# Decoder layer on one core: float32 products on raw data for the first two head pairs, and copies of products placed among the weight splits

## The chip, the cores and the metric

The kernel runs on one core of a Trainium2 chip. The metric is the device time in microseconds of one execution. Beside it one execution was taken by the hardware profiler; times within the kernel are microseconds from the start of that execution's span. The engines are PE (TensorE; PEld is its weight load), DVE (VectorE), ACT (ScalarE), POOL (GpSimd) and SP (SyncE, which only issues transfers here).

## The reference

One decoder layer over x of 8 batches x 128 tokens x 128 features, float32, with layer norms after each part:

```python
x = layernorm(x + self_attention(x))          # 16 heads of 64, causal
x = layernorm(x + cross_attention(x, ctx))    # 16 heads of 8, masked, with biases
x = layernorm(x + mixture(x))                 # 8 experts of 256, top-2 gates, all computed

# the part that matters here, in self_attention:
q = einsum('bsd,hqd->bhsq', x, w_q)
k = einsum('bsd,hqd->bhsq', x, w_k)
v = einsum('bsd,hvd->bhsv', x, w_v)
weights = softmax(causal(einsum('bhsq,bhtq->bhst', q, k)) / sqrt(64))
```

## The kernel before

All five engines run programs of their own, each in an order written out by hand, and wait for one another on semaphores. Batches are taken in pairs of 256 tokens for the q and k projections; p counts the eight pairs of heads (128 columns of w_q and of w_k each). `first_qk(p, b)` projects the first pair of batches into the PSUM bank b, q in its first 256 columns and k in its last 256; `next_qk` does the later pairs of batches, `project_v` one batch and half of the columns of w_v.

A projection is a split product. Each float32 operand is written as a rounded part (hi, in the format fp32r) and the rest (lo), and three fast products are summed: hi x hi, hi x lo, lo x hi (`split_product`, L1443 to L1445). The splitting is shared out:

- POOL splits x, two batches at a time: `split_x(k)` casts `x_hi` (L287) and subtracts `x_lo` (L289).
- ACT rounds the weights: `round_w(part)` (L515) writes `w_hi` and scales q's weights by 1/8. There are nine parts: columns 0 to 255 of q, of k, columns 256 to 511 of q, of k, and so on, and last the 1024 columns of w_v.
- DVE subtracts: `lower_w(part)` (L806) writes `w_lo`.

PE may start p = 2 when `w_lo_done` has reached 4, p = 4 at 6 and p = 6 at 8. Before its first projection PE multiplies a zeroed tile, `x1`, with itself WARM = 10 times (L1611). Copies of a product out of PSUM are shared by ACT (even p, L535) and DVE (odd p, L900). ACT does its eight roundings, then copies p = 0 and p = 2, then rounds w_v, then copies p = 4. DVE does eight subtractions, copies p = 1 and p = 3, subtracts w_v, then takes the maxima of the first two groups of scores (`group_max`, L839), copies v (`evac_v`, L915) and so on. `score_s(0, 0)` needs the copies of p = 0 to 3; `score_s(0, 1)`, in the bank OC from which `evac_v(0, 1)` copies, waits for that copy (`v_evac[1]`) and for the copies of p = 4 to 7. Scores go through `group_max`, `exp` (ACT, L525), a reciprocal (DVE, L846), `normalise` (POOL, L311) and `turn` (a transpose on PE, L1545).

Transfers go out in the order in which SP and ACT issue them: SP loads the first 256 tokens of xT, w_k's first columns, w_q's other three, w_v, the rest of xT, ctx, small weights and w_o. ACT loads w_q's first columns, w_k's other three, later the mask and x. When all nine lower parts are done SP issues the expert weights into the same memory.

PE's order is:

```python
for i in range(WARM): pe.matmul(OC[:, 0:P], x1[:], x1[:], start=True, stop=True)
first_qk(0, Y1); first_qk(1, OS); first_qk(2, T0); first_qk(3, T1)
first_qk(4, Y0); first_qk(5, X0)
score_s(0, 0, Y1, T1)
first_qk(6, X1)
project_v(0, 0, OS)
pe.wait_ge(maxed["s"][0], 1)
first_qk(7, Y1); next_qk(0, 0, T0)
project_v(0, 1, OC)
```

It goes on with `next_qk(0, 2)`, `next_qk(0, 3)`, `score_s(0, 1)`, `turn("s", 0, 0)`, `project_cv` (L1497, float32 products of 128 columns), and further on `turn("s", 2, 0)` and `turn("s", 3, 0)`, which stand at 23.1 us.

Of the kernel before, what the change touches and what calls it, by code (L numbers as in the profile page):

```python
# [9 lines left out]
ALU = mybir.AluOpType  # L10
ACT = mybir.ActivationFunctionType
AX_X = mybir.AxisListType.X

P = 128
# [24 lines left out]
def build_decoder(nc, x, xT, ctxT, mask, wqT, wkT, wvT, woT, cwqT, cwkT, cwvT, cwoT, cbq, cbk, cbv, cbo,  # L39
# [22 lines left out]
    W_PARTS = [(i, cols) for cols in W_COLS for i in (0, 1)] + [(2, slice(0, 1024))]  # L62
    NWP = len(W_PARTS)
    WARM = 10
# [9 lines left out]
    with ExitStack() as ctx:  # L74
# [3 lines left out]
        def sem(name):  # L78
            return ctx.enter_context(nc.semaphore(name))
# [130 lines left out]
        def hid_of(b):  # L210
            return max((j + 1 for j in range(NFILL) if FILL_BANK[j] is b), default=0)

        ld_xT, ld_xT_rest, ld_wv, ld_cwk, ld_cwq, ld_x, ld_ctx, ld_mask, ld_wo, ld_cw, ld_gu, ld_down = [
            sem(f"ld_{n}") for n in "xT xT_rest wv cwk cwq x ctx mask wo cw gu down".split()]
# [7 lines left out]
        ld_wqk = [sem(f"ld_w{'qk'[i]}{k}") for k in range(len(W_COLS)) for i in (0, 1)]  # L222
# [26 lines left out]
        def _(sp):  # L249
            sp.dma_start(xT_all[:, 0:2 * S], xT[:, 0:2 * S]).then_inc(ld_xT, 16)  # L250
            sp.dma_start(w_raw[:, 1, W_COLS[0]], wkT[:, W_COLS[0]]).then_inc(ld_wqk[1], 16)
            for k in range(1, len(W_COLS)):
                sp.dma_start(w_raw[:, 0, W_COLS[k]], wqT[:, W_COLS[k]]).then_inc(ld_wqk[2 * k], 16)
            sp.dma_start(w_raw[:, 2, :], wvT).then_inc(ld_wv, 16)
            sp.dma_start(xT_all[:, 2 * S:B * S], xT[:, 2 * S:B * S]).then_inc(ld_xT_rest, 16)
# [13 lines left out]
            sp.wait_ge(w_lo_done, NWP)  # L269
            sp.dma_start(gu_raw[:, 0, :], gateT).then_inc(ld_gu, 16)  # L270
# [12 lines left out]
        def _(pool):  # L283
            def split_x(k):
                toks = slice(2 * k * S, 2 * (k + 1) * S)
                pool.wait_ge(ld_xT if k == 0 else ld_xT_rest, 16)
                pool.tensor_copy(x_hi[:, toks], xT_all[:, toks]).then_inc(x_split, 1)  # L287
                pool.wait_ge(x_split, 2 * k + 1)
                pool.tensor_tensor(x_lo[:, toks], xT_all[:, toks], x_hi[:, toks].bitcast(F32), ALU.subtract).then_inc(x_split, 1)  # L289
# [217 lines left out]
        def _(act):  # L507
# [4 lines left out]
            def round_w(part_of):  # L512
                i, cols = W_PARTS[part_of]
                act.wait_ge((*ld_wqk, ld_wv)[part_of], 16)
                act.activation(w_hi[:, i, cols], w_raw[:, i, cols], ACT.Copy, scale=W_SCALE[i]).then_inc(w_hi_done, 1)  # L515
# [16 lines left out]
            def evac_first_qk(p, b):  # L532
                act.wait_ge(qk_first, p + 1)
                dst = qk_b[:, :, p % 4, :] if p >= 4 else qk_a[:, 0, :, p, :]
                act.copy(dst, b[:].rearrange("p (a c) -> p a c", a=2)).then_inc(qk_first_a, 1)  # L535
# [58 lines left out]
            round_w(1)  # L594
            round_w(2)
            round_w(3)
            round_w(4)
            round_w(5)
            round_w(6)
            round_w(7)  # L600
            evac_first_qk(0, Y1)
            evac_first_qk(2, T0)
            round_w(8)
            evac_first_qk(4, Y0)
# [193 lines left out]
        def _(dve):  # L798
# [4 lines left out]
            def lower_w(part_of):  # L803
                i, cols = W_PARTS[part_of]
                dve.wait_ge(w_hi_done, part_of + 1)
                dve.scalar_tensor_tensor(out=w_lo[:, i, cols], in0=w_raw[:, i, cols], scalar=W_SCALE[i],  # L806
                                         in1=w_hi[:, i, cols].bitcast(F32), op0=ALU.mult,
                                         op1=ALU.subtract).then_inc(w_lo_done, 1)
# [88 lines left out]
            def evac_first_qk(p, b):  # L897
                dve.wait_ge(qk_first, p + 1)
                dst = qk_b[:, :, p % 4, :] if p >= 4 else qk_a[:, 0, :, p, :]
                dve.tensor_copy(dst, b[:].rearrange("p (a c) -> p a c", a=2)).then_inc(qk_first_v, 1)  # L900
# [148 lines left out]
            lower_w(1)  # L1049
            lower_w(2)  # L1050
            lower_w(3)
            lower_w(4)
            lower_w(5)
            lower_w(6)
            lower_w(7)
            evac_first_qk(1, OS)
            evac_first_qk(3, T1)
            lower_w(8)
            dve.wait_ge(consts, 3)
            group_max("s", 0, 0, Y1)  # L1060
            group_max("s", 1, 0, T1)
            evac_v(0, 0, OS)
# [377 lines left out]
        def _(pe):  # L1440
# [13 lines left out]
            def first_qk(p, b):  # L1454
                if p == 0:

                    for a in range(2):
                        dst, cols = b[:, a * 2 * S:(a + 1) * 2 * S], slice(0, P)
                        pe.wait_ge(w_hi_done, a + 1)
                        pe.wait_ge(x_split, 1)  # L1460
                        pe.matmul(dst, w_hi[:, a, cols], x_hi[:, 0:2 * S], start=True, stop=False)
                        pe.wait_ge(x_split, 2)
                        pe.matmul(dst, w_hi[:, a, cols], x_lo[:, 0:2 * S], start=False, stop=False)
                        pe.wait_ge(w_lo_done, a + 1)
                        last = pe.matmul(dst, w_lo[:, a, cols], x_hi[:, 0:2 * S], start=False, stop=True)
                    last.then_inc(qk_first, 1)
                    return
                if p % 2 == 0:
                    pe.wait_ge(w_lo_done, p + 2)
                project_qk(0, p, b).then_inc(qk_first, 1)  # L1470
# [6 lines left out]
            def project_v(n, c, b):  # L1477
                if n == 0:
                    pe.wait_ge(w_lo_done, NWP)
# [638 lines left out]
```

## Time and profile before

| | |
|---|---|
| median of 3 runs | 233.37 us (233.29 to 233.5) |
| profiled execution, its own time | 233.06 us |
| its span | 231.0 us |
| PE, DVE, ACT, POOL busy | 98%, 83%, 71%, 44% |
| granted TensorE clock | 1.0 in the whole span |

A row of the timeline gives the start, the time from the first start to the last end of the instructions merged into it, the engine, the line of the kernel, the operation with what it writes and reads, how many instructions were merged, and in square brackets how long the engine had been idle before and who released it. PE's products overlap, so the pace of its stream is read from starts, not from lengths. A float32 product appears as two passes, each with a weight load.

### The profile page before, as it was taken

The page shows a single profiled execution, that of the slowest core. Times are in us where ns is not written, and L with a number is a line of the kernel's source. Part 1 is how long each engine was busy: PE and PEld are TensorE (multiplying, and loading weights), DVE is VectorE, ACT ScalarE, POOL GpSimd, SP SyncE. Part 2 cuts the span into 40 slices and gives each one's busy share as a digit, 9 for nine tenths or more (in the row PEclk, how much of TensorE's full clock was granted, in tenths as well). Part 3 has the DMA queues.
Part 4 walks back from the last instruction along what each step waited for, and adds up shares of the span by engine and source line. Part 5 has one row for each costly group of instructions (what it writes and reads, how often), then busy time and mean ns, then how long its engine had stood idle before and what let it go on. Part 6 is the DMA issues. An engine that isn't in the chain of part 4 may idle for free.

```text
span 231.0 us, 6982 instructions
## 1 busy us (share of the span) xinstructions
PE 225.9 (98%) x2274; PEld 205.9 (89%) x2274; DVE 192.1 (83%) x954; ACT 164.9 (71%) x552; POOL 102.0 (44%) x162
## 2 busy tenths in 40 slices
PE   8999999999999999999999999999999999999992
PEld 8999888997978988978978988789999999999992
DVE  3897798997889889989899879989898565766984
ACT  3768988898999979999989999697476333333001
POOL 4387738796396568922978351231200000100112
PEclk9999999999999999999999999999999999999999
DMA  6998000000000000000002200000000000000000
GB/s 189 362 363 314 10 0 0 4 3 1 3 1 3 0 6 3 0 3 1 1 4 64 121 3 3 3 0 4 0 3 0 1 3 0 4 23 0 26 23 24
DMA packets 7011, 9.10 MB, mean 39 GB/s; under 512 B 1088, under 2 KB 5824, under 8 KB 6592
## 3 DMA queue, kind: packets, MB, share of 16 engines
q1 hardware_dynamic: 4320, 7.09, 8.7%
q10 hardware_dynamic: 2656, 1.57, 2.3%
q8 instruction: 18, 0.29, 0.5%
q14 instruction: 17, 0.14, 0.2%
HBM read 8.14 MB, written 0.52 MB: 37 GB/s over the span
## 4 chain that ended last, share of the span: by engine, by line
PE 96%; DVE 1%; issue 1%; POOL 1%; ACT 0%; POOLq 0%; ACTq 0%; DVEq 0%
PE bank L1545 13%; PE bank L1443 11%; PE bank L1445 10%; PE bank L1444 10%; PE bank L2043 9%; PE bank L1527 7%; PE bank L1554 7%; PE bank L1595 6%; PE bank L1563 4%; PE bank L1538 3%; PE bank L1611 2%; PE bank L1482 2%; PE bank L1483 2%; PE bank L1484 2%; PE bank L1570 2%; PE bank L2053 1%
## 5 line engine op out<-in xcount | busy, mean ns | idle before, releaser
L525 ACT ACTIVATE probs_s<-masked_s,nmax_s 128x128 f32<-128x128 f32 x128 | 49.8, 396 | 3.6 <-DVE nmax_s L839 2.1
L311 POOL TENSOR_TENSOR probs_s<-probs_s,rec_sum_s 128x512 f32<-128x512 f32 x32 | 33.1, 1040 | 35.0 <-DVE rec_sum_s L846 34.8
L586 ACT ACTIVATE silu<-bank 128x256 f32<-128x256 f32 x54 | 20.1, 384 | 30.3 <-PE bank L1445 28.4
L528 ACT ACTIVATE probs_c<-masked_c,nmax_c 128x128 f32<-128x128 f32 x128 | 40.3, 396 | 1.6 <-DVE nmax_c L839 1.4
L1443 PE MATMUL bank<-ctx_hi,gu_hi 128*128 128x256 f32 x128 | 38.7, 302 | 0.0
L1444 PE MATMUL bank<-ctx_lo,gu_hi 128*128 128x256 f32 x128 | 35.7, 279 | 0.0
L1445 PE MATMUL bank<-ctx_hi,gu_lo 128*128 128x256 f32 x128 | 35.7, 279 | 0.0
L839 DVE CUSTOM_DVE_ANT_0 masked_c<-bank,mask_add 128x128 f32<-128x128 f32 x128 | 29.0, 286 | 4.6 <-PE bank L1538 3.9
L839 DVE CUSTOM_DVE_ANT_0 masked_s<-bank,causal 128x128 f32<-128x128 f32 x128 | 29.2, 285 | 1.2 <-PE bank L1527 1.0
L503 POOL TENSOR_TENSOR mv<-mv,minus_half 128x1 f32<-128x1 f32 x7 | 3.8, 556 | 55.2 <-DVE mv L1388 55.2
L1443 PEld LDWEIGHTS bank<-ctx_hi,gu_hi 128*128 128x128 f32 x128 | 24.3, 190 | 0.7 <-DVE qk_a L969 0.3
L525 ACT ACTIVATION_READ_ACCUMULATOR probs_s<-masked_s,nmax_s 128x1 f32 x128 | 24.8, 193 | 0.0
L1444 PEld LDWEIGHTS bank<-ctx_lo,gu_hi 128*128 128x128 f32 x128 | 24.1, 188 | 0.0
L1445 PEld LDWEIGHTS bank<-ctx_hi,gu_lo 128*128 128x128 f32 x128 | 24.0, 188 | 0.0
L567 ACT COPY xT_all<-bank 128x512 f32<-128x512 f32 x32 | 17.8, 580 | 2.6 <-PE bank L1545 1.5
L1545 PE MATMUL bank<-ident,probs_c 128*128 128x128 f32 x128 | 18.8, 275 | 0.0
L1545 PE MATMUL bank<-ident,probs_s 128*128 128x128 f32 x128 | 18.7, 276 | 0.0
L1443 PE MATMUL bank<-x_hi,w_hi 128*128 128x256 f32 x62 | 18.2, 293 | 0.0
L969 DVE TENSOR_TENSOR qk_a<-silu,bank 128x256 f32<-128x256 f32 x32 | 12.7, 419 | 6.5 <-ACT silu L586 6.2
L1554 PE MATMUL bank<-probsT_s,v_sb 128*64 128x128 f32 x256 | 17.5, 279 | 0.0
L1445 PE MATMUL bank<-x_hi,w_lo 128*128 128x256 f32 x62 | 17.3, 279 | 0.0
L1444 PE MATMUL bank<-x_lo,w_hi 128*128 128x256 f32 x62 | 17.3, 279 | 0.0
(180 smaller groups left out, 591.4 us busy)
## 6 DMA issues: line engine op xcount, KB each, us to landing
raw<-in_gateT SPq DMA_DIRECT2D x1, 1024.0 KB, 8.2
raw<-in_upT SPq DMA_DIRECT2D x1, 1024.0 KB, 12.1
down_sb<-in_down SPq DMA_DIRECT2D x1, 1024.0 KB, 5.2
raw<-in_wvT SPq DMA_DIRECT2D x1, 512.0 KB, 5.6
ctxT_all<-in_ctxT SPq DMA_DIRECT2D x1, 512.0 KB, 6.9
masked_c<-in_mask ACTq DMA_DIRECT2D x1, 512.0 KB, 11.9
wo_sb<-in_woT SPq DMA_DIRECT2D x1, 512.0 KB, 6.1
x_tok<-in_x ACTq DMA_DIRECT2D x1, 512.0 KB, 11.2
```

The lines of the kernel that those rows point to most:

```text
L311: pool.tensor_tensor(probs_s[:, g % 2], probs_s[:, g % 2], spread(rec_sum_s[:, 4 * g:4 * g + 4], 2, S), ALU.mult).then_inc(normed[g], 1)
L525: last = act.activation(probs_s[:, g % 2, i, :], masked_s[:, g % 2, i, :], ACT.Exp, scale=-1.0, bias=nmax_s[:, h:h + 1], accum_out=rsum_s[ ...
L528: last = act.activation(probs_c[:, g % 2, i, :], masked_c[:, g % 2, i, :], ACT.Exp, scale=-1.0, bias=nmax_c[:, h:h + 1])
L567: act.copy(dst[:, g % 2].rearrange("p h t -> p (h t)"), b[:]).then_inc(turned_evac[kind][g], 1)
L586: act.activation(silu[:, i % NS, :], g, ACT.Silu).then_inc(silued, 1)
L839: last = dve.tensor_tensor_reduce(out=masked[:, g % 2, i, :], in0=b[:, i * S:(i + 1) * S], in1=add, scale=-1.0, scalar=3e38, op0=ALU.add, ...
L1443: pe.matmul(dst, wh, xh, start=True, stop=False)
L1444: pe.matmul(dst, wh, xl, start=False, stop=False)
L1445: return pe.matmul(dst, wl, xh, start=False, stop=True)
L1545: last = pe.transpose(b[:, i * S:(i + 1) * S], (probs_s if kind == "s" else probs_c)[:, g % 2, i, :], ident[:])
L1554: last = pe.matmul(b[DQ * r:DQ * (r + 1), i * S:(i + 1) * S], v_sb[:, 8 * a + 2 * i + r, :], probsT_s[:, r, i, :], start=True, stop=True)
L2043: last = pe.matmul(down_bank(ce)[:, tb * P:(tb + 1) * P], hid[c % 2][:, e * FB + fb, tb * P:(tb + 1) * P], down_sb[:, e * FB + fb, :], sta ...
```

## The change

For p = 0 and 1, `first_qk` multiplies the loaded weights and the loaded xT in float32, one product for q and one for k instead of three each, and waits for the loads alone. Their copies out of PSUM scale q by 1/8. The parts of weights are now ordered columns 256, 512, 768 and then 0 (these are needed by the later pairs of batches), and w_v is split in two halves. The copies of the first products stand among the roundings and subtractions, and the subtraction for the second half of w_v stands behind the first two `group_max`. The next 256 tokens of xT are loaded ahead of w_v, the dummies are 7 and not 10, and PE waits for `w_lo_done` 2, 4 and 6 ahead of p = 2, 4 and 6, for 9 and 10 ahead of the halves of v.

```diff
-    W_PARTS = [(i, cols) for cols in W_COLS for i in (0, 1)] + [(2, slice(0, 1024))]
+    W_PARTS = [(i, k) for k in (1, 2, 3, 0) for i in (0, 1)] + [(2, 0), (2, 1)]
+    NDIRECT = 2
+
+    def w_cols(i, k):
+        return W_COLS[k] if i < 2 else slice(512 * k, 512 * (k + 1))
     NWP = len(W_PARTS)
-    WARM = 10
+    WARM = 7
...
-        ld_wqk = [sem(f"ld_w{'qk'[i]}{k}") for k in range(len(W_COLS)) for i in (0, 1)]
+        ld_wqk = [sem(f"ld_w{'qk'[i]}{k}") for k in range(2) for i in (0, 1)]
+
+        for k in (2, 3):
+            ld_wqk += 2 * [sem(f"ld_wqk{k}")]
...
+            sp.dma_start(xT_all[:, 2 * S:4 * S], xT[:, 2 * S:4 * S]).then_inc(ld_xT_next, 16)
             sp.dma_start(w_raw[:, 2, :], wvT).then_inc(ld_wv, 16)
-            sp.dma_start(xT_all[:, 2 * S:B * S], xT[:, 2 * S:B * S]).then_inc(ld_xT_rest, 16)
+            sp.dma_start(xT_all[:, 4 * S:B * S], xT[:, 4 * S:B * S]).then_inc(ld_xT_rest, 16)
...
             sp.wait_ge(w_lo_done, NWP)
+            sp.wait_ge(qk_first, NDIRECT)
...
-                pool.wait_ge(ld_xT if k == 0 else ld_xT_rest, 16)
+                pool.wait_ge((ld_xT, ld_xT_next, ld_xT_rest, ld_xT_rest)[k], 16)
...
             def evac_first_qk(p, b):
...
-                act.copy(dst, b[:].rearrange("p (a c) -> p a c", a=2)).then_inc(qk_first_a, 1)
+                if p < NDIRECT:
+                    act.activation(dst[:, 0], b[:, 0:2 * S], ACT.Copy, scale=W_SCALE[0])
+                    act.copy(dst[:, 1], b[:, 2 * S:4 * S]).then_inc(qk_first_a, 1)
+                else:
+                    act.copy(dst, b[:].rearrange("p (a c) -> p a c", a=2)).then_inc(qk_first_a, 1)
...
             round_w(0)
             round_w(1)
+            evac_first_qk(0, Y1)
             round_w(2)
             round_w(3)
             round_w(4)
             round_w(5)
+            evac_first_qk(2, T0)
             round_w(6)
             round_w(7)
-            evac_first_qk(0, Y1)
-            evac_first_qk(2, T0)
             round_w(8)
+            round_w(9)
             evac_first_qk(4, Y0)
...
+                if p < NDIRECT:
+                    dve.tensor_scalar(dst[:, 0], b[:, 0:2 * S], W_SCALE[0], None, ALU.mult)
+                    dve.tensor_copy(dst[:, 1], b[:, 2 * S:4 * S]).then_inc(qk_first_v, 1)
...
             lower_w(0)
             lower_w(1)
+            evac_first_qk(1, OS)
             lower_w(2)
             lower_w(3)
-            lower_w(4)
-            lower_w(5)
-            lower_w(6)
-            lower_w(7)
-            evac_first_qk(1, OS)
             evac_first_qk(3, T1)
-            lower_w(8)
+            for part_of in range(4, NWP - 1):
+                lower_w(part_of)
             dve.wait_ge(consts, 3)
             group_max("s", 0, 0, Y1)
             group_max("s", 1, 0, T1)
+            lower_w(NWP - 1)
             evac_v(0, 0, OS)
...
             def first_qk(p, b):
-                if p == 0:
-
-                    for a in range(2):
-                        dst, cols = b[:, a * 2 * S:(a + 1) * 2 * S], slice(0, P)
-                        pe.wait_ge(w_hi_done, a + 1)
-                        pe.wait_ge(x_split, 1)
-                        pe.matmul(dst, w_hi[:, a, cols], x_hi[:, 0:2 * S], start=True, stop=False)
-                        pe.wait_ge(x_split, 2)
-                        pe.matmul(dst, w_hi[:, a, cols], x_lo[:, 0:2 * S], start=False, stop=False)
-                        pe.wait_ge(w_lo_done, a + 1)
-                        last = pe.matmul(dst, w_lo[:, a, cols], x_hi[:, 0:2 * S], start=False, stop=True)
+                if p < NDIRECT:
+
+                    if p == 0:
+                        pe.wait_ge(ld_xT, 16)
+                    for i in range(2):
+                        if p % 2 == 0:
+                            pe.wait_ge(ld_wqk[p + i], 16)
+                        last = pe.matmul(b[:, i * 2 * S:(i + 1) * 2 * S], w_raw[:, i, p * P:(p + 1) * P], xT_all[:, 0:2 * S],
+                                         start=True, stop=True)
                     last.then_inc(qk_first, 1)
                     return
+                if p == NDIRECT:
+                    pe.wait_ge(x_split, 2)
                 if p % 2 == 0:
-                    pe.wait_ge(w_lo_done, p + 2)
+                    pe.wait_ge(w_lo_done, p - NDIRECT + 2)
                 project_qk(0, p, b).then_inc(qk_first, 1)
...
                 if n == 0:
-                    pe.wait_ge(w_lo_done, NWP)
+                    pe.wait_ge(w_lo_done, NWP - 1 + c)
```

## Rows read from the trace of the kernel before

**Rows 1.** The page: busy time by engine, and the chain that ended last.

```profile
PE 225.9 (98%) x2274; PEld 205.9 (89%) x2274; DVE 192.1 (83%) x954; ACT 164.9 (71%) x552; POOL 102.0 (44%) x162
...
PE 96%; DVE 1%; issue 1%; POOL 1%; ACT 0%; POOLq 0%; ACTq 0%; DVEq 0%
```

**Rows 2.** Timeline of PE and its weight loads, 0 to 8.5 us.

```profile
0.98 4.64 PE L1611 MATMUL bank<-x 128*128 128x128 f32 x20 [0.98 <-POOL x L381]
...
5.20 0.33 PEld L1461 LDWEIGHTS bank<-x_hi,w_hi 128*128 128x128 f32 x1
...
5.78 0.19 PEld L1461 LDWEIGHTS bank<-x_hi,w_hi 128*128 128x128 f32 x1
...
6.82 0.27 PE L1445 MATMUL bank<-x_hi,w_lo 128*128 128x256 f32 x1
...
7.00 0.38 PE L1443 MATMUL bank<-x_hi,w_hi 128*128 128x256 f32 x1
...
8.40 0.28 PE L1445 MATMUL bank<-x_hi,w_lo 128*128 128x256 f32 x1
```

**Rows 3.** Timeline of POOL, ACT and DVE, 3.5 to 11.4 us.

```profile
3.78 0.40 POOL L287 CAST x_hi<-xT_all 128x256 fp32r<-128x256 f32 x1 [1.46 <-DMA xT_all<-in_xT]
...
4.26 0.73 POOL L289 TENSOR_TENSOR x_lo<-xT_all,x_hi 128x256 fp32r<-128x256 f32 x1
...
5.74 2.06 ACT L515 ACTIVATE w_hi<-raw 128x256 fp32r<-128x256 f32 x6 [0.70 <-DMA raw<-in_wqT]
...
6.19 2.15 DVE L806 SCALAR_TENSOR_TENSOR w_lo<-raw,w_hi 128x256 fp32r<-128x256 f32 x6 [0.58 <-ACT w_hi L515]
...
7.70 1.05 ACT L535 COPY qk_a<-bank 128x512 f32<-128x512 f32 x2
...
8.25 1.28 DVE L900 COPY qk_a<-bank 128x512 f32<-128x512 f32 x2
...
9.74 1.36 DVE L806 SCALAR_TENSOR_TENSOR w_lo<-raw,w_hi 128x1024 fp32r<-128x1024 f32 x1 [0.21 <-ACT w_hi L515]
...
10.10 1.59 POOL L289 TENSOR_TENSOR x_lo<-xT_all,x_hi 128x256 fp32r<-128x256 f32 x1
...
11.33 0.29 DVE L839 CUSTOM_DVE_ANT_0 masked_s<-bank,causal 128x128 f32<-128x128 f32 x1 [0.23 <-PE bank L1527]
```

**Rows 4.** Transfers by issue, windows up to 3.5 us: size, us to landing.

```profile
raw<-in_wqT ACTq DMA_DIRECT2D x1, 128.0 KB, 3.2
...
raw<-in_wqT SPq DMA_DIRECT2D x1, 128.0 KB, 4.1
...
raw<-in_wvT SPq DMA_DIRECT2D x1, 512.0 KB, 5.6
```

**Rows 5.** The chain that ended last, 0 to 60 us: start, length, what.

```profile
17.95 1.79 PE bank L1497 x16
```

**Rows 6.** Timelines of PE, DVE, ACT and POOL, 14 to 24 us; waits to 30 us.

```profile
14.90 0.69 DVE L915 COPY v_sb<-bank 128x512 f32<-128x512 f32 x1
...
16.20 1.16 PE L1527 MATMUL bank<-qk_b 64*128 64x128 f32 x16
...
18.47 0.40 ACT L525 ACTIVATE probs_s<-masked_s,nmax_s 128x128 f32<-128x128 f32 x1
...
20.27 0.40 ACT L525 ACTIVATE probs_s<-masked_s,nmax_s 128x128 f32<-128x128 f32 x1 [0.15 <-PE bank L1545]
...
22.21 1.04 POOL L311 TENSOR_TENSOR probs_s<-probs_s,rec_sum_s 128x512 f32<-128x512 f32 x1 [0.76 <-DVE rec_sum_s L846]
...
23.11 1.09 PE L1545 MATMUL bank<-ident,probs_s 128*128 128x128 f32 x8
...
DVE rec_sum_s L846 <- ACT probs_s L525: 2.6, 4, 1.0
```

**Rows 7.** Instructions of L806, two windows: count, ns min/median/max, first and last start.

```profile
L806 DVE SCALAR_TENSOR_TENSOR w_lo<-raw,w_hi x1: 899/899/899, 4.4 to 4.4; 128x256 fp32r<-128x256 f32 x1
...
L806 DVE SCALAR_TENSOR_TENSOR w_lo<-raw,w_hi x6: 418/419/426, 6.2 to 7.9; 128x256 fp32r<-128x256 f32 x6
```

More of the change, by code:

```diff
@@ L211, in hid_of @@
             return max((j + 1 for j in range(NFILL) if FILL_BANK[j] is b), default=0)
-        ld_xT, ld_xT_rest, ld_wv, ld_cwk, ld_cwq, ld_x, ld_ctx, ld_mask, ld_wo, ld_cw, ld_gu, ld_down = [
-            sem(f"ld_{n}") for n in "xT xT_rest wv cwk cwq x ctx mask wo cw gu down".split()]
+        ld_xT, ld_xT_next, ld_xT_rest, ld_wv, ld_cwk, ld_cwq, ld_x, ld_ctx, ld_mask, ld_wo, ld_cw, ld_gu, ld_down = [
+            sem(f"ld_{n}") for n in "xT xT_next xT_rest wv cwk cwq x ctx mask wo cw gu down".split()]
         stored, consts, pad_set, mask_set, w_hi_done, w_lo_done, gu_split, x_split, ctx_hi_done, ctx_lo_done, cwk_ready, cwq_ready, bias_step, bias_then_mean = [
@@ L512, in round_w @@
             def round_w(part_of):
-                i, cols = W_PARTS[part_of]
-                act.wait_ge((*ld_wqk, ld_wv)[part_of], 16)
+                i, k = W_PARTS[part_of]
+                cols = w_cols(i, k)
+                act.wait_ge(ld_wqk[2 * k + i] if i < 2 else ld_wv, 32 if i < 2 and k >= 2 else 16)
                 act.activation(w_hi[:, i, cols], w_raw[:, i, cols], ACT.Copy, scale=W_SCALE[i]).then_inc(w_hi_done, 1)
@@ L803, in lower_w @@
             def lower_w(part_of):
-                i, cols = W_PARTS[part_of]
+                i, cols = W_PARTS[part_of][0], w_cols(*W_PARTS[part_of])
                 dve.wait_ge(w_hi_done, part_of + 1)
@@ L899, in evac_first_qk @@
                 dst = qk_b[:, :, p % 4, :] if p >= 4 else qk_a[:, 0, :, p, :]
-                dve.tensor_copy(dst, b[:].rearrange("p (a c) -> p a c", a=2)).then_inc(qk_first_v, 1)
+                if p < NDIRECT:
+                    dve.tensor_scalar(dst[:, 0], b[:, 0:2 * S], W_SCALE[0], None, ALU.mult)
+                    dve.tensor_copy(dst[:, 1], b[:, 2 * S:4 * S]).then_inc(qk_first_v, 1)
+                else:
+                    dve.tensor_copy(dst, b[:].rearrange("p (a c) -> p a c", a=2)).then_inc(qk_first_v, 1)
             def evac_qk(n, i, b):
```

## The prediction

> **What bounds the kernel now.** I read the page first. PE is busy 98% of the span and 96% of the chain that ended last is PE [rows 1], so the end is set by when PE's stream of useful products starts and by the holes in it, not by the average load of DVE (83%), ACT or POOL. The reader should then follow PE alone from the start [rows 2]. Ten dummy products of x1 fill 0.98 to about 5.2; the first projection's weight load is at 5.20, its last product starts at 6.82, and the stream goes on at 7.00 after a hole of about 0.06 us (products of this form start every 0.117 us: p=2 and p=3, twelve products, from 7.00 to the last start at 8.40). From there on no hole in PE's starts is longer than 0.1 us until the scores at 16.20. So the whole question is whether the product at 7.00 comes earlier, and whether a new hole opens behind it.
>
> What gates 7.00? PE waits for the lower half of the second weight columns (cols 256 to 511) of q and k. DVE makes the two from 6.19 on; six such subtractions take 2.15 us, each 0.42, so they start every (2.15 - 0.42)/5 = 0.35 and the second ends at 6.19 + 0.35 + 0.42 = 6.96. DVE waits for ACT's rounding, which starts at 5.74 and had sat 0.70 us idle for the load of wqT [rows 3]. That load was issued at 1.63 and took 4.1 us: 5.73 [rows 4]. The gate of the stream is a transfer, and behind it a fixed chain of one rounding and two subtractions; PE itself is free at 6.94.
>
> **The change, part by part, with the sum.**
>
> *Seven dummies, direct float32 products of p=0 and 1.* The 20 passes of the ten dummies (128 columns, two passes each) start over some 4.2 us, 0.213 us each, and the weight load at 5.20 takes 0.33 us [rows 2]: the 1.2 GHz level. At 5.78 a load takes 0.19, the 2.4 GHz level; PE had been busy without a hole since 0.98. The granted clock column reads full all along, so only the durations show this. Seven dummies end at 0.97 + 14 x 0.213 = 3.95. xT has landed by 3.78, when POOL casts it [rows 3], wqT's first columns at 0.72 + 3.2 = 3.92 [rows 4], and wkT's by 4.62 at the latest (ACT's idle of 0.70 before 5.74 began at 5.04, after the rounding of these, 0.42 long). No float32 product of 256 columns is in the trace; I scale the passes: 2 x 2 x 0.213 = 0.85 us at 1.2 GHz; at 2.4 GHz the sixteen passes of cv (128 columns) take 1.79 us, 0.112 each [rows 5], so 0.45 us. Four products: 3.95, 4.8, 5.65, 6.1, done near 6.55. With the slow level throughout it would be 3.95 + 3.4 = 7.35. In place of an end at 6.94 this is 0.4 us sooner, and it buys nothing: p=2 still needs the same load at 5.73, rounded and subtracted by the same two engines, which did nothing else before it. Transfers ahead of it in both queues are unchanged. Value: 0.00 (bounds -0.4, if the load came as early as PE, +0.35). The direct products cost PE 4 x (0.45 to 0.85) where splits cost 4 x 0.35, but this lies under the wait.
>
> *Copies of products among the splits.* ACT: roundings every 0.33, copies of 512 columns every 0.48; the direct one is split in two, about 0.66. So 5.74 + 2 x 0.33 = 6.40, copy to 7.06, third and fourth rounding done 7.48 and 7.81. DVE: two subtractions to 6.91 (next start), two half copies of p=1 (a 512 copy starts the next after 0.60, a split one some 0.08 more; 0.66 taken) to 7.57, then subtractions 7.57 and 7.93, done 8.35. p=4 would start at 8.51: hidden, with 0.1 us to spare. DVE then waits for p=3 (8.7), copies to 9.30, four subtractions to 10.70, half of wv (about 0.68, next start after 0.61) to 11.33. That is when group_max starts now [rows 3], so the early part breaks even. p=6 needs its weights at 11.09 and they are there by 10.1. wv's load is a little later (512 KB, 5.6 us after 3.05, now behind 128 KB more of xT: about 9.0) and ACT comes to it at 9.5: hidden. project_v(0,0) at 11.90 needs 11.4: hidden.
>
> *The second half of wv, after the two group_max.* This is the piece with a price. It puts 0.61 us ahead of evac_v(0,0), evac_first_qk(5), evac_first_qk(7) and evac_v(0,1), between which DVE has no idle. evac_v(0,1) now runs 14.90 to 15.59; PE's scores need it at 16.20 (PE's turn would come at 16.11) [rows 6]. With 0.61 + 0.05 it ends at 16.25, scores at 16.29: +0.09 us. The same lateness passes through ACT: exp of group 2 starts at 18.47, as soon as its maximum is out; 0.66 later it ends near 20.8, so exp of group 3 starts 0.5 late instead of 20.27, POOL's normalise(3,0), now 22.21 to 23.25, ends at 23.75, and PE wants to turn it 0.44 after 23.11, at 23.55 [rows 6]. PE then is +0.22 behind. DVE sits idle 2.6 us in four places before its reciprocals in the first 30 us [rows 6], so its own lateness dies out; on PE it stays.
>
> *POOL beside DVE.* The next xT columns now land about 7.4 (issued in wv's place at 3.05, and the load before took 4.1 and its successors a little more [rows 4]), two us sooner than now, so POOL's cast (0.40) and subtraction (0.73) fall at 7.4 to 8.6, beside DVE's subtractions. The trace has both directions: POOL's subtraction took 1.59 instead of 0.73 beside DVE's big one, and DVE's first took 899 ns instead of 419 beside POOL's at 4.26 [rows 3, 7]. A cast costs DVE less: the 1024-column subtraction met the tail of one at 9.74 and took 1.36, where 419 ns plus 768 columns at 0.27 us per 256 (the 0.35 less about 0.08 of overhead) gives 1.22. The cast at 7.4 is taken at 0.2 us, which the wait for p=3 swallows on DVE (8.29 against 8.7). In the wv piece at 13.0 POOL is also at work on the last two pairs, as it is now; I take 0.15 us there (bounds 0 and 0.73, one whole subtraction).
> On this the Trainium skill, page SBUF — State Buffer, section "SBUF: two separate sides", says that whichever of a GpSimd op and a VectorE op with two SBUF inputs starts first takes the shared ports for its whole length and the other blocks; by that rule, the trace agrees (899 ns), and a subtraction of POOL that starts first would hold DVE 0.6 to 0.7 us, which is the rival below.
>
> Sum: 0.00 + 0.22 + 0.15 = +0.37 us. The profiled execution took 233.06 (span 231.0), 0.31 under the median of 233.37; so 233.43 for it and **233.74** as a median.
>
> The other transfers: the gate and up loads now wait for the last of wv's subtractions and start some 2.7 us later, and the mask's about one; what reads them comes more than 3 us (mask) and 10 us (gate, up) after they land now: hidden.
>
> **Rivals.** A change under 0.2% (0.47 us) can't be told from none here.
> - *POOL's subtraction comes first* (slower). Place: between lower_w(2) and (3) at 8.0, or ahead of the wv piece at 13.1. It decides when POOL's instruction is already waiting as DVE's ends. At 8.0 DVE loses 0.2 + 0.73; less the 0.41 of waiting, 0.5 remains, and p=4 starts 0.8 late; final +0.9 to +1.0. At 13.1 it is +0.22 + 0.73. Time 234.3, both together 234.9. For it: DVE's 899 ns. Against: DVE's subtractions follow each other without a gap and POOL pauses 0.08 us between cast and subtraction. 0.32.
> - *The clock rises later* (slower): with fewer dummies and a hole of some 0.45 us at 6.55, PE stays at 1.2 GHz to beyond 7.0, and the twelve products of p=2 and 3 start every 0.23 instead of 0.117: up to +1.4 us, 234.8. Against: PE is as busy as before until 6.5. 0.05.
> - *The stream starts earlier* (faster): if wqT's second columns landed by 5.3, p=2 would start at 6.6, -0.4, and 232.9 to 233.1. More than -0.47 needs the late copies to cost nothing and small waits further on to shrink. Nothing ahead of that load in its queue has changed. 0.13, a bit more than half of it beyond 0.2%.
> - *My sum*: 0.50, 233.5 to 233.95, of which 0.06 lies above 233.84.
>
> **Numbers.** Faster: 0.08. Slower: 0.32 + 0.05 + 0.06, less 0.02 of the first that ends small: 0.41. Same: 0.51. The range takes my case, most of the first rival (to 234.5) and the near end of the faster one: 232.95 to 234.5, leaving both subtractions lost, the late clock and a real gain outside.
>
> **What the profile after would show.** Weight loads of p=0 from about 3.95, of the long kind till 5.6; a hole of PE near 6.5 to 7.0, then p=2 at 7.0. If p=2 starts before 6.8, my gate is wrong. p=4 at 8.5, or 9.3 if POOL got between. DVE's subtractions at 419 ns or some at 0.6 to 1.1 us beside POOL's cast and subtraction from 7.4. group_max near 11.4; the wv piece at 13.1 and evac_v(0,1) ending near 16.3; scores of heads 8 to 15 at 16.4 instead of 16.20; normalise(3,0) ending near 23.9. The prediction fails most simply if the lateness of DVE is larger than 0.8 us at 16 us, or if DVE does not block at all.

## The result, and the profile after

| | before | after |
|---|---|---|
| median | 233.35 us (232.96 to 233.87, 20 executions) | 234.19 us (233.01 to 234.72, 20 executions) |
| profiled execution, its own time | 233.06 | 234.55 |
| its span | 231.0 | 232.5 |

The medians differ by 0.84 us. Over all executions the ratio is 1.0026, with a 95% interval of 1.0014 to 1.0039: slower by a quarter of a per cent, about 0.6 us. The time lies inside the range given, but on the slower side (0.41), not where the likeliest case had it (233.74, no difference to be told). The executions of the changed kernel fall into two groups, 7 of them from 233.01 to 233.57 and 13 from 233.89 to 234.72, with nothing in between; those of the kernel before form one group. The median of the changed kernel is one of the upper group, which is why the medians lie further apart than the ratio says. The lower group is no slower than the kernel before: its own median is 233.29.

The page after: busy time by engine, and the chain that ended last.

```profile
PE 226.2 (97%) x2264; PEld 204.8 (88%) x2264; DVE 192.4 (83%) x956; ACT 164.6 (71%) x554; POOL 101.6 (44%) x162
...
PE 90%; DVE 5%; DMA 2%; issue 1%; ACT 1%; POOL 0%; SPq 0%; POOLq 0%; DVEq 0%; ACTq 0%
```

No engine is busier than in [rows 1], yet DVE's share of the chain has gone from 1% to 5%. The first 18 us of that chain say where (start, length, what):

```profile
1.63 4.32 DMA raw<-in_wqT
5.98 0.43 ACT w_hi L526
6.43 0.76 DVE w_lo L822 x2
7.19 0.37 DVE qk_a L917
7.55 0.33 DVE qk_a L918
7.88 1.32 DVE w_lo L822 x2
9.25 0.39 PE bank L1461
...
12.18 0.29 DVE masked_s L855
...
13.96 1.11 DVE w_lo L822
15.07 0.60 DVE v_sb L935
15.68 0.60 DVE qk_b L920
16.36 0.58 DVE qk_b L920
16.93 0.61 DVE v_sb L935
17.59 1.16 PE bank L1545 x16
```

The reader should see that the stream of products no longer sets the pace here: DVE does, from its first subtraction to p = 4, and again from the maxima to the scores of heads 8 to 15. A DVE instruction that is lengthened in these stretches lengthens the kernel by as much as it makes PE wait. The timeline (DVE, POOL, PE) shows two that are long:

```profile
7.80 1.39 DVE L822 SCALAR_TENSOR_TENSOR w_lo<-raw,w_hi 128x256 fp32r<-128x256 f32 x2
13.88 1.20 DVE L822 SCALAR_TENSOR_TENSOR w_lo<-raw,w_hi 128x512 fp32r<-128x512 f32 x1
7.64 0.40 POOL L297 CAST x_hi<-xT_all 128x256 fp32r<-128x256 f32 x1 [3.00 <-DMA xT_all<-in_xT]
8.12 0.79 POOL L299 TENSOR_TENSOR x_lo<-xT_all,x_hi 128x256 fp32r<-128x256 f32 x1
13.79 0.73 POOL L299 TENSOR_TENSOR x_lo<-xT_all,x_hi 128x256 fp32r<-128x256 f32 x1
7.33 0.36 PE L1461 MATMUL bank<-x_hi,w_hi 128*128 128x256 f32 x1 [0.24 <-DVE w_lo L822]
9.25 0.39 PE L1461 MATMUL bank<-x_hi,w_hi 128*128 128x256 f32 x1 [0.27 <-DVE w_lo L822]
```

Both lie under a split of x by POOL. Taken one instruction at a time (count, ns min/median/max, first and last start):

```profile
L822 DVE SCALAR_TENSOR_TENSOR w_lo<-raw,w_hi x1: 517/517/517, 7.8 to 7.8; 128x256 fp32r<-128x256 f32 x1
...
L822 DVE SCALAR_TENSOR_TENSOR w_lo<-raw,w_hi x1: 954/954/954, 8.2 to 8.2; 128x256 fp32r<-128x256 f32 x1
...
L822 DVE SCALAR_TENSOR_TENSOR w_lo<-raw,w_hi x1: 1195/1195/1195, 13.9 to 13.9; 128x512 fp32r<-128x512 f32 x1
```

Undisturbed, the first two take 419 ns [rows 7]. The first was held by POOL's cast, the second by its subtraction from 8.12 to 8.91: it ended 0.3 us after that, at about 9.2. I call 7.8 the first meeting and 13.9 the second.

Four steps sum up a trace: the start of p = 2, of p = 4, of the scores of heads 8 to 15, and of the turn at [rows 6]'s 23.11.

| profiled execution | own time | span | p = 2 | p = 4 | scores | turn |
|---|---|---|---|---|---|---|
| before | 233.06 | 231.0 | 7.00 | 8.51 | 16.20 | 23.11 |
| after | 234.55 | 232.5 | 7.33 | 9.25 | 17.59 | 24.50 |

From the scores to the turn there are 6.91 us in both; the span less the scores is 214.8 and 214.9. So the whole loss of this execution is made by 17.6 us: 0.74 us ahead of p = 4, and 0.65 between p = 4 and the scores. Of the 0.74, 0.33 is the later start of p = 2. The other 0.41 is a hole in PE's stream: from p = 2 to p = 4 there are 1.51 us in before, where twelve products follow one another without a wait, and 1.92 in after.

These two executions differ by 1.49 us, more than the medians do, since the one of before is among the faster of its kernel and the one of after among the slower.

### The profile page after: what moved, and what is told of

Same layout as the page of the kernel before. It is cut to its first block, busy times and chain, and to the rows that moved or that the text cites. A ratio compares the mean times of both kernels' runs of the same rounds, so it can differ in the third digit from the quotient of the medians.

```text
span 232.5 us, 6968 instructions
## 1 busy us (share of the span) xinstructions
PE 226.2 (97%) x2264; PEld 204.8 (88%) x2264; DVE 192.4 (83%) x956; ACT 164.6 (71%) x554; POOL 101.6 (44%) x162
## 3 DMA queue, kind: packets, MB, share of 16 engines
HBM read 8.14 MB, written 0.52 MB: 37 GB/s over the span
## 4 chain that ended last, share of the span: by engine, by line
PE 90%; DVE 5%; DMA 2%; issue 1%; ACT 1%; POOL 0%; SPq 0%; POOLq 0%; DVEq 0%; ACTq 0%
PE bank L1563 13%; PE bank L1461 10%; PE bank L2061 9%; PE bank L1462 9%; PE bank L1463 9%; PE bank L1545 7%; PE bank L1572 7%; PE bank L1613 6%; PE bank L1581 4%; PE bank L1556 3%; DMA raw<-in_wqT 2%; PE bank L1500 2%; PE bank L1588 2%; PE bank L1502 1%; PE bank L1501 1%; DVE w_lo L822 1%
## 5 line engine op out<-in xcount | busy, mean ns | idle before, releaser
L1461 PE MATMUL bank<-x_hi,w_hi 128*128 128x256 f32 x60 | 17.7, 295 | 0.5 <-DVE w_lo L822 0.5
L1463 PE MATMUL bank<-x_hi,w_lo 128*128 128x256 f32 x60 | 16.8, 280 | 0.0
L1462 PE MATMUL bank<-x_lo,w_hi 128*128 128x256 f32 x60 | 16.8, 279 | 0.0
```

Of the source, the lines that this page charges most:

```text
L1461: pe.matmul(dst, wh, xh, start=True, stop=False)
L1462: pe.matmul(dst, wh, xl, start=False, stop=False)
L1463: return pe.matmul(dst, wl, xh, start=False, stop=True)
```

## The experiments

Times are medians. Kernels under one heading ran on one chip and share its runs of the kernel before (first heading 233.40, second 233.21, third 233.32).

### Holding POOL back at the first meeting, at the second, at both; the products alone

e2_first_clear, in `split_x`, behind the wait for the load:

```diff
+                if k == 1:
+                    pool.wait_ge(w_lo_done, NWP - 1)
```

> The changed kernel, with only the first meeting taken away: POOL's split of the second pair of batches waits for the ninth subtraction of DVE. Theory A: no hole ahead of p=4 (0.47 us in the profile of the changed kernel), 234.19 less 0.3 to 0.5 = 233.7 to 233.9; POOL is later, so the meeting at 14 us may be longer. Rivals B and C: 234.1 to 234.3.

e3_second_clear, with `normalise("s", 0, 0)` placed ahead of `split_x(3)`:

```diff
+                if k == 2:
+                    pool.wait_ge(w_lo_done, NWP)
```

> The changed kernel, with only the second meeting taken away: POOL's split of the third pair of batches waits for the tenth subtraction. Theory A: the last subtraction takes 0.69 us and not 1.20, scores of the other eight heads start 0.3 to 0.5 us earlier, median 233.7 to 233.9; the hole ahead of p=4 stays in some runs. Rivals B and C: 234.1 to 234.3.

e1_clear has both waits, one more for `w_lo_done` NWP ahead of the first split of ctx, and the same swap:

```diff
+                if k in (1, 2):
+                    pool.wait_ge(w_lo_done, NWP - 2 + k)
```

> The changed kernel, but POOL's splits of x are kept away from DVE's subtractions of weights: the split of the second pair of batches waits for the ninth subtraction, the first rounding of ctx for the tenth, and one normalise goes ahead of the last split. Theory A (the time is lost where POOL's and DVE's instructions with two inputs in SBUF block each other, at 8 us and at 14 us): every 256-column subtraction takes about 0.42 us and the last one about 0.69, p=4 starts within 0.1 us of p=3's last product, and the median is 233.5 to 233.7 against 233.35 before, with a spread of single runs under 1 us. Rival B (the loads of the weights land later, p=2 starts 0.3 late, and this is what costs): 234.0 to 234.3, still with a wide spread. Rival C (it is the work of the last subtraction behind the maxima, block or no block): 233.9 or more.

e4_direct_alone is the kernel before with the float32 products of p = 0 and 1, their scaled copies and seven dummies, every order left as it was:

```diff
-    WARM = 10
+    WARM = 7
...
+                if p < 2:
+                    if p == 0:
+                        pe.wait_ge(ld_xT, 16)
+                    for i in range(2):
+                        if p % 2 == 0:
+                            pe.wait_ge(ld_wqk[p + i], 16)
+                        last = pe.matmul(b[:, i * 2 * S:(i + 1) * 2 * S], w_raw[:, i, p * P:(p + 1) * P], xT_all[:, 0:2 * S],
+                                         start=True, stop=True)
```

> The kernel before, with only the float32 products of p=0 and 1 and seven dummies; order of the parts, loads and copies as before. If the prediction's step holds that the direct products buy nothing and cost nothing since p=2 waits for the load of its weights, its rounding and two subtractions: 233.3 to 233.5, p=2 at 7.0 to 7.1 in the profile. If an early load of q's or k's first columns being late (5.5 us instead of 4.6 in the profile after) is a consequence of PE reading raw data or of fewer dummies: p=2 at 7.3 and 233.6 to 233.7. If the direct products do buy time: under 233.1.

| | median | ratio to before, 95% | p = 2 | p = 4 | scores | span |
|---|---|---|---|---|---|---|
| e2_first_clear | 233.28 | 0.9999 (0.9988 to 1.0009) | 7.11 | 8.79 | 16.73 | 231.7 |
| e3_second_clear | 233.71 | 1.0011 (0.9999 to 1.0023) | 7.24 | 9.25 | 17.09 | 232.1 |
| e1_clear | 233.85 | 1.0015 (1.0003 to 1.0027) | 7.18 | 8.66 | 16.38 | 231.6 |
| e4_direct_alone | 233.50 | 1.0006 (0.9994 to 1.0018) | 6.65 | 8.14 | 16.11 | 231.2 |

e2 can't be told from before: one wait gives the whole loss back. But it does not clear the first meeting alone. POOL's later splits come later too, and at the second meeting DVE is now the first (timeline of e2_first_clear, DVE and POOL):

```profile
13.42 0.80 DVE L824 SCALAR_TENSOR_TENSOR w_lo<-raw,w_hi 128x512 fp32r<-128x512 f32 x1
13.75 1.07 POOL L301 TENSOR_TENSOR x_lo<-xT_all,x_hi 128x256 fp32r<-128x256 f32 x1
```

DVE's piece takes 0.80 us here, and 1.20 in the changed kernel. So e2 prices both meetings together. e3 clears the second (the piece takes 0.69) and leaves the first (1.31 us for the two subtractions). It is 0.11% slower than before, with an interval that just reaches no change and overlaps that of the changed kernel: perhaps half of the loss is back, and the first meeting alone costs at most 0.23%, or 0.54 us. No run prices either meeting more closely.

Clearing both by three waits (e1) should have been best and was a miss: on the same chip it is slower than e2, with 233.85 against 233.28. Its trace shows most of the reason: by the scores only 0.18 of the 1.39 us is left, but POOL's held-back work runs into what comes next (timeline of e1_clear, POOL, DVE and weight loads):

```profile
22.83 1.04 POOL L325 TENSOR_TENSOR probs_s<-probs_s,rec_sum_s 128x512 f32<-128x512 f32 x1 [0.48 <-DVE rec_sum_s L866]
...
18.87 0.61 POOL L308 CAST ctx_hi<-ctxT_all 128x512 fp32r<-128x512 f32 x1
...
18.93 1.09 DVE L833 TENSOR_TENSOR ctx_lo<-ctxT_all,ctx_hi 128x512 fp32r<-128x512 f32 x1
...
23.99 0.42 PEld L1567 LDWEIGHTS bank<-ident,probs_s 128*128 128x128 f32 x4 [0.28 <-issue]
```

A cast by POOL now meets DVE's subtraction for ctx, which takes 1.09 us where its next takes 0.71. `normalise(3, 0)` ends at 22.83 + 1.04 = 23.87, and the second half of the turn starts behind it, 0.28 us late at 23.99: that is the wait which the prediction put there, met here and not in the changed kernel. Its span is 231.6, 0.6 more than before's; the median is no better than e3's.

e4 shows what the float32 products buy by themselves. p = 2 started 0.35 us sooner in its profile. The load behind it was early there (ACT rounded it from 5.29 on, and from 5.74 in before), and PE, done with the float32 products, could use that; in before PE is busy until 6.94. The lead was partly eaten at the first scores, which waited 0.20 us for a copy by DVE; the kernel's time can't be told from before.

### The load of x alone, its undoing, p = 5 on ACT, and the changed kernel again

after_again is the changed kernel once more.

> The changed kernel once more, beside the others. Theory A (POOL and DVE block each other where they happen to meet): again a wide spread, some runs near 233.3 and the rest 234.1 to 234.7, since each meeting is won by one engine or the other; in a profile, the run's time goes with the lengths of DVE's subtractions at 8 and at 14 us: none longer than 0.8 us in a run near 233.3, two in one near 234.5. Rival B (late loads): the time goes with the start of p=2 alone, whatever the lengths are.

e5_early_x is the kernel before with nothing but the load of the next 256 tokens placed ahead of w_v:

```diff
+            sp.dma_start(xT_all[:, 2 * S:4 * S], xT[:, 2 * S:4 * S]).then_inc(ld_xT_next, 16)
             sp.dma_start(w_raw[:, 2, :], wvT).then_inc(ld_wv, 16)
```

> The kernel before, with only the load of the next 256 tokens of xT moved ahead of w_v, so that POOL splits them at 7.4 to 8.6 instead of from 9.6. Theory A: this part alone makes POOL's subtraction meet the run of DVE's subtractions; one of the fourth to eighth takes 0.9 to 1.1 us, the copies of p=1 and p=3 come 0.4 to 0.7 later, scores start 0.2 to 0.3 later than 10.0, median 233.5 to 233.9. If the meeting matters only in the new order: 233.3 to 233.4.

e7_late_x is the changed kernel with that load back behind w_v:

```diff
-            sp.dma_start(xT_all[:, 2 * S:4 * S], xT[:, 2 * S:4 * S]).then_inc(ld_xT_next, 16)
             sp.dma_start(w_raw[:, 2, :], wvT).then_inc(ld_wv, 16)
-            sp.dma_start(xT_all[:, 4 * S:B * S], xT[:, 4 * S:B * S]).then_inc(ld_xT_rest, 16)
+            sp.dma_start(xT_all[:, 2 * S:B * S], xT[:, 2 * S:B * S]).then_inc(ld_xT_rest, 16)
```

> The changed kernel, with the load of xT in its old place behind w_v, so that POOL's split of the second pair comes at 9.6 to 11 and no hole stands ahead of p=4. Theory A: POOL now meets DVE's subtractions five to nine (9.3 to 11.4) instead of three and four, so the loss moves: p=4 on time, but the maxima 0.2 to 0.7 later in part of the runs; 233.4 to 234.1, not all of the 0.84 back. If only the first meeting's place matters for PE: 233.3 to 233.5, as with POOL's first split held back.

e8_p5_on_act is e2 with the copy of p = 5 on ACT, behind that of p = 4, in place of DVE, and with PE's waits for copies counted to match.

> The changed kernel with POOL's second split held back until the ninth subtraction (233.28 against 233.40 before in the run before), and in addition the copy of p=5 made by ACT, which waits 1.5 us for the maxima there, and not by DVE. If DVE's lateness of 0.6 us in front of evac_v(0,1) still costs PE at the scores of the other eight heads (they started 7.94 after p=4, in the kernel before 7.69): 0.1 to 0.3 less, 233.0 to 233.2, faster than before. If PE's stream alone is the bound: 233.2 to 233.4.

| | median | ratio to before, 95% | p = 2 | p = 4 | scores | span |
|---|---|---|---|---|---|---|
| after_again | 233.82 | 1.0029 (1.0012 to 1.0045) | 7.10 | 8.93 | 17.28 | 232.2 |
| e5_early_x | 233.81 | 1.0024 (1.0011 to 1.0036) | 7.58 | 8.98 | 17.11 | 232.0 |
| e7_late_x | 234.59 | 1.0051 (1.0034 to 1.0069) | 7.29 | 9.06 | 18.07 | 232.9 |
| e8_p5_on_act | 233.62 | 1.0014 (1.0004 to 1.0025) | 6.84 | 8.34 | 16.03 | 231.2 |

The changed kernel repeats its loss, and its two groups (six executions up to 233.46, six from 234.18). e5, with one moved load, has it almost in full (0.24%). Its timeline (DVE, POOL, PE):

```profile
7.34 2.21 DVE L807 SCALAR_TENSOR_TENSOR w_lo<-raw,w_hi 128x256 fp32r<-128x256 f32 x4 [0.68 <-ACT w_hi L516]
8.14 0.80 POOL L290 TENSOR_TENSOR x_lo<-xT_all,x_hi 128x256 fp32r<-128x256 f32 x1
10.90 0.57 PE L1528 MATMUL bank<-qk_a 64*128 64x128 f32 x5 [0.36 <-DVE qk_a L901]
```

Four subtractions took 2.21 us; where nothing meets them, in e4, four take 1.43. The 0.78 us is one subtraction by POOL, and PE waits 0.36 us for the copy behind it. The scores at 10.90 are 0.90 us later than in before (10.00); the other 0.54 comes from a later p = 2 (PE's products started every 0.21 us, the 1.2 GHz level, until about 7.1 us). So in this one profile the late clock moved PE by more than the meeting did, and how the two share the loss of the median isn't shown.

It doesn't follow that the early load is to be undone. e7's timeline (DVE, POOL, PE):

```profile
9.60 3.17 DVE L821 SCALAR_TENSOR_TENSOR w_lo<-raw,w_hi 128x256 fp32r<-128x256 f32 x5
14.38 1.18 DVE L821 SCALAR_TENSOR_TENSOR w_lo<-raw,w_hi 128x512 fp32r<-128x512 f32 x1
10.01 0.59 POOL L296 CAST x_hi<-xT_all 128x256 fp32r<-128x256 f32 x1 [5.31 <-DMA xT_all<-in_xT]
10.68 0.79 POOL L298 TENSOR_TENSOR x_lo<-xT_all,x_hi 128x256 fp32r<-128x256 f32 x1
15.61 0.50 PE L1499 MATMUL bank<-w_hi,x_hi 128*128 128x512 f32 x1 [0.28 <-DVE w_lo L821]
```

The first meeting is gone, but POOL's split now falls among the five subtractions, which take 3.17 us where 2.02 is clean: more is lost than in the changed kernel, and it is the slowest kernel of all (six executions). e8 was a miss: it was to be no slower than e2, and is 0.14% slower than before, with an interval clear of no change. Its own profile has the scores at 16.03, sooner than before, but is of its fastest execution (233.16). What its other executions lose isn't shown.

### e2 once more, and four float32 pairs

> The changed kernel with POOL's second split held back until the ninth subtraction, once more. Theory A: within 0.2% of the kernel before, on its good side or bad (first time 0.9999 of it), and 0.5 to 0.9 us below the changed kernel (1.0026 and 1.0029 of before). If the first time was luck: 1.002 or more.

e9_four_direct is e2 with `NDIRECT = 4` and `pe.wait_ge(w_lo_done, p)` ahead of p = 4 and 6.

> As the one before it, and p=2 and 3 as float32 products of the raw data too (p=4 still waits for four subtractions). If PE's wait for rounding and subtraction ahead of p=2 is all that keeps the gain of the early start away: p=2 starts as soon as its load has landed (5.3 to 6.0), p=3 is copied 0.4 us earlier by DVE, and the time falls 0.2 to 0.5 us under the kernel with two direct pairs. If DVE's chain of subtractions is the next bound (p=4 at 8.3 to 8.5 in any case) or PE's slower float32 products eat it, above all in runs in which the clock rises late: equal within 0.2 us, or slower.

| | median | ratio to before, 95% | p = 4 | scores | span |
|---|---|---|---|---|---|
| e2_again | 233.33 | 1.0003 (0.9993 to 1.0013) | 8.25 | 16.05 | 231.0 |
| e9_four_direct | 233.51 | 1.0009 (1.0000 to 1.0017) | 8.40 | 16.22 | 231.3 |

The timeline of e2_again (DVE, POOL) is what the clean kernel looks like:

```profile
7.20 0.75 DVE L824 SCALAR_TENSOR_TENSOR w_lo<-raw,w_hi 128x256 fp32r<-128x256 f32 x2
9.06 2.02 DVE L824 SCALAR_TENSOR_TENSOR w_lo<-raw,w_hi 128x256 fp32r<-128x256 f32 x5
12.78 0.76 DVE L824 SCALAR_TENSOR_TENSOR w_lo<-raw,w_hi 128x512 fp32r<-128x512 f32 x1
11.22 0.40 POOL L299 CAST x_hi<-xT_all 128x256 fp32r<-128x256 f32 x1 [6.57 <-DVE w_lo L824]
```

It equals before a second time. The last piece takes 0.76 us: here too the second meeting is gone with the first. With four pairs PE multiplies without a hole from 4.12 us on, in sixteen passes that take 4.40 us, and reaches p = 4 no sooner; the time is at best that of before, and by the interval up to 0.17% longer. No version tried beats the kernel before.

All these runs take the meetings away or move them. None made POOL's subtraction longer to see the loss grow.

### Two more profiles of the changed kernel

The first two profiles of it were both of the upper group, so there are two more.

> The changed kernel as it is, one more profiled execution. Its times come in two clumps, 233.0 to 233.6 and 233.9 to 234.9; the two profiles so far are both of the upper one. Theory: the clumps are who goes first where POOL's split of the second two batches meets DVE's subtractions of parts 2 and 3. So an execution under 233.6 shows DVE's part 3 at 0.42 to 0.52 us with POOL's x_lo lengthened behind it (over 1.2 us instead of 0.73), p=4 at 8.5 to 8.6 and scores of heads 8 to 15 at 16.5 to 16.9; one above 233.9 shows a subtraction of 0.9 us or more and p=4 at 8.9 or later. Rival: the clumps are the load of wqT's second columns, so that p=2's start (7.0 against 7.3) carries the difference and the subtractions look alike in both.

> The same kernel once more, for the same question: under 233.6 POOL waits for DVE at the first meeting and p=4 starts at 8.5 to 8.6; above 233.9 DVE waits for POOL and p=4 starts at 8.9 or later. Rival: both look alike there and differ in p=2's start.

look_a took 233.49 us, in the lower group. Its timeline (DVE, POOL, PE):

```profile
7.85 0.76 DVE L822 SCALAR_TENSOR_TENSOR w_lo<-raw,w_hi 128x256 fp32r<-128x256 f32 x2 [0.49 <-ACT w_hi L526]
13.28 0.84 DVE L822 SCALAR_TENSOR_TENSOR w_lo<-raw,w_hi 128x512 fp32r<-128x512 f32 x1
8.19 0.67 POOL L297 CAST x_hi<-xT_all 128x256 fp32r<-128x256 f32 x1 [3.63 <-DMA xT_all<-in_xT]
13.65 1.06 POOL L299 TENSOR_TENSOR x_lo<-xT_all,x_hi 128x256 fp32r<-128x256 f32 x1
8.66 0.38 PE L1461 MATMUL bank<-x_hi,w_hi 128*128 128x256 f32 x1 [0.18 <-DVE w_lo L822]
```

Here the loads were later: x landed at 8.19 and not 7.64, so both subtractions of the first meeting were under way or done, and the instruction that was held was POOL's cast (0.67 in place of 0.40). At the second meeting DVE was first too: its piece took 0.84, and POOL's subtraction 1.06 in place of 0.73. p = 4 started at 8.66, the scores at 16.63, the span was 231.5. The engines did meet once more, since POOL's subtraction now stood at 8.94:

```profile
9.13 2.45 DVE L822 SCALAR_TENSOR_TENSOR w_lo<-raw,w_hi 128x256 fp32r<-128x256 f32 x5
```

The five take 2.02 in e2_again; the first of them took 839 ns. Nothing was lost by it, because the maxima behind them wait for PE's scores: they start at 11.58, some 0.2 us after these end, as they do in the changed kernel's first profile.

look_b took 234.06, in the upper group:

```profile
7.36 0.42 DVE L917 TENSOR_SCALAR qk_a<-bank 128x256 f32<-128x256 f32 x1 [0.83 <-PE bank L1480]
8.03 1.02 DVE L822 SCALAR_TENSOR_TENSOR w_lo<-raw,w_hi 128x256 fp32r<-128x256 f32 x2
13.74 1.06 DVE L822 SCALAR_TENSOR_TENSOR w_lo<-raw,w_hi 128x512 fp32r<-128x512 f32 x1
7.70 0.74 POOL L299 TENSOR_TENSOR x_lo<-xT_all,x_hi 128x256 fp32r<-128x256 f32 x1
9.11 0.39 PE L1461 MATMUL bank<-x_hi,w_hi 128*128 128x256 f32 x1 [0.37 <-DVE w_lo L822]
```

POOL was first at both places again, though at the first it cost 0.27 us (1.02 less 0.75). The rest of its late p = 4 is another wait: DVE sat idle 0.83 us for p = 1, whose float32 products were slow. Their passes (count, ns min/median/max, first and last start) took mostly 634 ns, against mostly 379 in the changed kernel's first profile:

```profile
L1480 PE MATMUL bank<-xT_all,raw x8: 379/634/634, 4.1 to 6.9; 128*128 128x256 f32 x8
```

Here are the four profiles of the changed kernel side by side. The piece is DVE's subtraction at the second meeting.

| profile | own time | p = 2 | p = 2 to p = 4 | piece | p = 4 to scores | scores |
|---|---|---|---|---|---|---|
| before | 233.06 | 7.00 | 1.51 | | 7.69 | 16.20 |
| after | 234.55 | 7.33 | 1.92 | 1.20 | 8.34 | 17.59 |
| after_again | 234.27 | 7.10 | 1.83 | 1.20 | 8.35 | 17.28 |
| look_b | 234.06 | 6.97 | 2.14 | 1.06 | 8.21 | 17.32 |
| look_a | 233.49 | 6.84 | 1.82 | 0.84 | 7.97 | 16.63 |

The order of the engines goes with the group, as expected: POOL first at both places in the upper three, DVE first in the lower one. But the first meeting does not separate them well. look_a has a hole ahead of p = 4 too, 0.31 us, though nothing held DVE's subtractions there: DVE sat idle 0.49 us before them for ACT, which waited for a later load. Only look_b needs clearly longer to p = 4 (0.32 more than look_a). What all three of the upper group have over look_a is the second meeting, 0.24 to 0.38 us between p = 4 and the scores, and a start of p = 2 that is 0.13 to 0.49 later. The rival, that p = 2 alone carries the difference, fails in look_b, where it is 0.13 of the 0.69 us at the scores; in the first profile it is half (0.49 of 0.96). Three executions of the upper group and one of the lower are few.

## Why the prediction was wrong in its likeliest case

**What bounds the kernel.** Right for before. The four profiles of the changed kernel have p = 2 at 7.33, 7.10, 6.97 and 6.84, around the 7.00 that the load, a rounding and two subtractions were to give. The value of 0.00 for the direct products holds, within the spread of that load: the chain of waits shows it at 4.32 us after, and it took 3.76 in e2_again.

**The float32 products.** One took about 0.45 us at the faster level as scaled: with PE at the 2.4 GHz level for all but their start, four take 2.0 us in look_a, from 4.12. The prediction priced a late rise of the clock by p = 2 and 3, at 0.05. It did come late in look_b (to about 6.9 us), and the products behind it were fast; what it cost was DVE's wait for p = 1. The prediction counted only PE's own products behind the rise, not DVE, whose subtractions for p = 4 stand behind the copy of p = 1. It also had w_k's first columns landed by 4.62; in the first profile PE waited for them until 5.53, and had done the four products in time for p = 2 all the same.

**Copies among the splits.** Right within 0.3 us where nothing meets them: p = 4 at 8.25 (e2_again) to 8.79 (e2_first_clear), for 8.51 forecast. The 0.1 us to spare was too little for a late load, as in look_a.

**The second half of w_v.** Sized at +0.09 at the scores. From p = 4 to the scores there are 7.69 us in before, and 7.72 to 7.97 in the four traces where the piece took 0.69 to 0.84 us (e1, e2_again, e2_first_clear, look_a): +0.03 to +0.28. The second part of that term, +0.13 more through `normalise(3, 0)`, didn't come: the turn stood 6.91 us behind the scores in before and after alike. e2, which has this piece and pays next to nothing at the meetings, should by this term be 0.22 us (0.09%) slower than before, and measured 0.9999 and 1.0003 of it. The term is rather too large; the intervals, which reach 1.0009 and 1.0013, don't rule it out.

**POOL beside DVE: the step that failed.** The prediction said of it: "The cast at 7.4 is taken at 0.2 us, which the wait for p=3 swallows on DVE", and of the piece at 13: "I take 0.15 us there". Measured after, against e2_again: 1.39 for 0.75 and 1.20 for 0.76, or 0.64 and 0.44 us. Of the first 0.41 reached PE, the second reached it in full. At the first place PE waits for the second of these subtractions itself (p = 4), ahead of the wait for p = 3. The mechanism was on the list, as the rival "POOL's subtraction comes first", with both its places and +0.9 to +1.0 for the first; what was off was its weight, 0.32, against 0.50 for the sum. The argument against it was that DVE's subtractions have no gap and POOL pauses 0.08 us between its two. It doesn't hold: POOL was first at both places in three profiles of four. Four terms make up the first profile's 1.39 us at the scores: 0.33 for the late p = 2, 0.41 for the hole that the first meeting makes, 0.44 for the second, and 0.21 left for the w_v piece (0.65 less 0.44). The whole is close to what the rival gave for both places together (234.9, or 1.5 us over before; the two profiled executions differ by 1.49). It had its parts wrong: it counted no late load, and 0.22 for the piece.

The Trainium skill, page SBUF — State Buffer, section "SBUF: two separate sides", has the pair of ports held for a whole instruction by whichever of a GpSimd op and a VectorE op with two SBUF inputs starts first. The traces agree on who holds whom, in both directions: DVE's 954 ns beside POOL's subtraction, POOL's cast at 0.67 and subtraction at 1.06 us behind DVE in look_a. They don't agree to the end of the record: waiting until DVE's instruction ends would make these two 0.82 and 1.20.

**The forecast time.** No execution took 233.74: it lies in the gap between the two groups. The lower group, 14 of the 34 executions of the changed kernel, is at the level of before (medians of 233.29 and 233.32 where before had 233.35 and 233.21; look_a 233.49), so for it the forecast of +0.37 was too much. The upper group lies about 1 us above before. The range holds because it took in most of the rival to which the prediction gave 0.32, not because its sum was right.

**Shown, and not shown.** Shown by undoing it: with the one wait the kernel equals before, twice, and both long subtractions are gone from its profiles. So the meetings together cost the quarter of a per cent; what each costs alone isn't shown. Shown by doing it alone: the moved load is enough for a loss of 0.24%; that it comes by the meeting is read from one profile, in which the clock was late too. Not settled: what makes the loads and the rise of the clock vary from run to run; whether every execution of the upper group has lost at a meeting; and where the gain goes that e2_again's and e8's profiles show at the scores (0.15 us and more). In both executions it is still there at 39 us (a product with `k_own` starts at 39.30 and 39.28, for 39.45 in before), and yet the spans are 231.0 and 231.2, for 231.0 in before.

## What to carry to other kernels

Before crediting a faster start, look at which engine's chain the new order puts in front of PE, and whether that engine has any idle time left: here PE's wait moved to DVE, with 0.1 us to spare, and DVE's delays reached PE. A load that is moved earlier also moves the work that waits for it; place it by what that work will run beside, and if it is POOL's, keep it off the two-input DVE instructions that others wait for, with a semaphore if need be. One such wait, with no change in the amount of work, was worth a quarter of a per cent (about 0.6 us); holding back more than that one piece made the kernel slower again. Read in the profile what else such a wait moves: this one was meant for one meeting and cleared two.

## What the runs showed of the hardware beyond what was expected

POOL gets in between DVE subtractions that follow each other without a gap: in after the first, 517 ns, ends at about 8.3, and the second waits for a POOL instruction that started at 8.12. A cast, with one input, held DVE too: 517 ns for 419. The same load of 128 KB took 3.76 us to land in e2_again and 4.32 in after. And PE left the 1.2 GHz level by 5.78 us in before [rows 2] but only at about 7.1 in e5, whose PE program is the same, with the granted clock shown as full there in both.
